# Weighting expert outputs before they are stored, and adding them to X inside the gathering transfers

## The chip, the cores and the metric

The program runs on one core of a Trainium2 chip. The metric is device time in microseconds (us). Six things work side by side: TensorE (PE in the profile; its weight loads are PEld), VectorE (DVE), ScalarE (ACT), GpSimd (POOL), SyncE (SP), which issues transfers, and 16 DMA engines. Transfers issued by SP appear in the profile as queue q1, those issued by ACT as q10 and those issued by POOL as q0. Each engine works through its instructions in order, and semaphores tie the engines together.

## What is computed

The model has two layers on X, 2048 tokens (4 sequences of 512) of 512 values. Each layer adds a state-space block and a feed-forward block to X. The feed-forward block of the first layer is a mixture of experts, and this is the part that the change touches:

```
router_logits = x @ gate_w.T                        # 16 experts
routing_weights = softmax(router_logits)
topk_w, topk_ids = top_k(routing_weights, 4)
def body(acc, ew):                                  # for each of the 16 experts e
    coef = sum(where(topk_ids == e, topk_w, 0.0), axis=-1)
    h = silu_and_mul(x @ w13_e.T)                   # 2 x 352 wide
    acc = acc + (h @ w2_e.T) * coef[:, None]
out = shared + sparse_out                           # shared: a dense expert, 1408 wide
```

The feed-forward block of the second layer quantizes its three weight matrices to -1, 0 or 1, with one scale per matrix (the mean absolute value of the whole matrix), and its activations to integers.

## The kernel before

Tokens stand in 16 tiles of 128 (`TT` = 16); X stays in SBUF as `X[128, 16, 512]` through the program. The program is a row of blocks, with a barrier and the clearing of that block's semaphores (`Mem.clear`) between two of them:

1. `ssm_first`: the state-space block of layer 0; beside it the expert weights are split into two half-precision parts.
2. `gate` for layer 0: multiplies by the gate, adds to X, normalizes, computes the router's logits.
3. `routing`: softmax, the four best experts of each token, and for each (token, choice) its place in a table of 80 x 128 slots (`NSTEP` = 80 steps of 128 slots, each step with one expert). DVE works out `r["pos"]`, the slot of each (token, choice), by a chain of small instructions. Then comes the inverse table `r["idx"]`, the token of each slot. It is built in a loop over the 64 pairs g of a token tile i and a choice k: DVE writes two one-hot matrices, `ohp` (L1007, 128 x 128, which row inside a step) and `ohs` (L1008, 128 x 80, which step, times the token's number), and PE adds their product to `pi` in PSUM (L1034). Four buffers of each let DVE run at most four pairs ahead; the semaphores are `oh_rdy` and `oh_used`. A float32 matmul is two passes in the trace, so 64 of them show as 128. Behind the loop DVE does some one-row arithmetic for the tables of weights (L1011 to L1019) and copies `pi` out (L1022).
4. `experts_and_ssm`: the shared expert and then 80 expert steps, with the state-space block of layer 1 spread over them. Step g fetches 128 tokens by `r["idx"]`, and its result stands in `py`. `y_evac(g)` on ACT (L1349) copies it to `yo` with a constant scale, and `y_store(g)` writes it to `y_d` in HBM, not weighted.
5. `combine`: two jobs that share a block. One is to add to X the 64 gathers, again one per pair g = (tile i, choice k), i outer: POOL issues an indirect transfer of 128 rows of `y_d` to one of 8 buffers `yr` (L1558), and DVE multiplies by the token's weight `w8` and adds to X (L1614). POOL waits for a free buffer (`used`), DVE for the landing (`got`). The other job quantizes the weights of layer 1: SP loads 12 pieces of 1 MB (L1550), DVE sums the magnitudes of each (L1592), then come the three totals (L1597), a matmul over partitions (L1566) and the scales (L1601, L1603); only then can the pieces be converted, each by ACT (L1571), DVE (L1607, `clip`) and ACT (L1581). DVE's order between the two jobs is written out by hand: a magnitude after each of the gathers 1 to 12, then a clip after every third.
6. `gate` for layer 1, and `quant_ffn`, the last block, which needs X, the quantized weights and their scales.

## Time and profile before

| what | us |
|---|---|
| three runs | 2286.73, 2280.6, 2284.96; median 2284.96 |
| the profiled execution, its own time | 2281.42 |
| its span, first to last instruction | 2279.2 |
| `routing`, by the trace | 723.3 to 785.3 |
| `experts_and_ssm` | 785.3 to 1906.0 |
| `combine` | 1906.0 to 2029.5 |
| `gate` and `quant_ffn` of layer 1 | 2029.5 to 2279.2 |

The profiled execution lies 3.5 us under the median of the runs, and its own time is 2.2 us over its span. Over the whole span the page gives PE 74% busy, DVE 77%, ACT 52% and POOL 59%, so no engine is the limit of everything. The blocks follow each other with barriers; a block's time is set by what ends last in it, and what a block gains or loses is passed on to the end.

### The profile page before, as it was taken

How to read it: one execution, taken by the hardware profiler on the slowest of the kernel's cores; microseconds unless marked ns; L12 is line 12 of the kernel's file. 1: busy time of each engine (PE TensorE's matmuls, PEld its weight loads, DVE VectorE, ACT ScalarE, POOL GpSimd, SP SyncE). 2: the span in 40 equal slices, each digit the busy share in tenths (PEclk: the TensorE clock that was granted, in tenths of full speed). 3: DMA queues.
4: the chain of work that ended last, by engine and by line, in shares of the span. 5: the costliest groups of instructions: out<-in, count | busy, mean ns of one | idle time of the engine just before them, and what ended most of it. 6: DMA issues, size and time to landing. Idle time of an engine off the chain costs nothing. (4 is left out here: it accounts for less than half of the span.)

```text
span 2279.2 us, 27596 instructions
## 1 busy us (share of the span) xinstructions
PE 1683.4 (74%) x8608; PEld 967.8 (42%) x8630; DVE 1759.7 (77%) x2275; ACT 1184.7 (52%) x1829; POOL 1336.8 (59%) x648
## 2 busy tenths in 40 slices
PE   4766756656536488999799988999889992005998
PEld 1222222212225445766467545666456661003554
DVE  4999999999955738887689847888478885757886
ACT  4675766757632034443444435555355551634776
POOL 0778778789950005775288815888258884653111
PEclk7878879889976588999899998999989996558999
DMA  6347456456544600001000333344424226650000
GB/s 213 132 149 236 149 169 222 152 177 223 182 143 134 144 24 10 11 13 35 5 10 30 135 113 137 121 157 159 144 95 157 81 75 249 210 170 1 24 24 28
DMA packets 127146, 264.65 MB, mean 116 GB/s; under 512 B 44546, under 2 KB 48386, under 8 KB 121794
## 3 DMA queue, kind: packets, MB, share of 16 engines
q1 hardware_dynamic: 93890, 184.24, 24.0%
q0 software_dynamic: 11520, 37.76, 5.8%
q10 hardware_dynamic: 21600, 40.90, 4.8%
q8 instruction: 78, 1.28, 0.2%
q14 instruction: 58, 0.48, 0.1%
HBM read 180.41 MB, written 82.44 MB: 115 GB/s over the span
## 5 line engine op out<-in xcount | busy, mean ns | idle before, releaser
L471 POOL TENSOR_TENSOR ssm_hs<-ssm_hs,ssm_Cs 128x1024 f32<-128x1024 f32 x128 | 314.9, 2461 | 144.7 <-DVE ssm_hs L434 140.7
L471 POOL TENSOR_TENSOR moe_hs<-moe_hs,moe_Cs 128x1024 f32<-128x1024 f32 x128 | 302.2, 2361 | 127.2 <-DVE moe_hs L434 96.1
L434 DVE TENSOR_TENSOR_SCAN moe_hs<-moe_dA,moe_bu 128x1024 f32<-128x1024 f32 x128 | 292.6, 2286 | 17.9 <-ACT moe_dA L348 8.4
L434 DVE TENSOR_TENSOR_SCAN ssm_hs<-ssm_dA,ssm_bu 128x1024 f32<-128x1024 f32 x128 | 292.8, 2287 | 17.4 <-ACT ssm_dA L348 0.5
L461 POOL TENSOR_TENSOR moe_U<-moe_U,moe_hs 128x1024 f32<-128x1024 f32 x128 | 302.0, 2360 | 5.9
L280 PE MATMUL ssm_pY<-ssm_hs,ssm_ident 128*128 128x512 f32 x512 | 276.9, 668 | 2.8 <-POOL ssm_hs L471 2.8
L1246 PE MATMUL moe_pgu<-all_Wreg,moe_xth 128*128 x1280 | 249.6, 318 | 31.4 <-DVE moe_xtl L1446 31.3
L1196 PE MATMUL moe_pgu<-moe_xsh,all_Wreg 128*128 128x256 f16 x1408 | 251.8, 277 | 10.9 <-DVE moe_hsl L1434 9.4
L258 PE MATMUL ssm_pB<-ssm_bc,ssm_sel 96*128 96x512 bf16 x128 | 54.9, 429 | 204.4 <-DVE ssm_bu L425 204.3
L1196 PE MATMUL moe_pgu<-moe_xsl,all_Wreg 128*128 128x256 f16 x704 | 195.0, 277 | 0.0
L666 POOL TENSOR_TENSOR ssm_wlo<-ssm_wst,ssm_whi 128x1360 f16<-128x1360 f32 x64 | 186.5, 2915 | 0.0
L348 ACT ACTIVATE ssm_dA<-ssm_dlt,ssm_A 128x511 f32<-128x511 f32 x256 | 169.0, 709 | 24.2 <-DVE ssm_hs L434 24.1
L348 ACT ACTIVATE moe_dA<-moe_dlt,moe_A 128x511 f32<-128x511 f32 x256 | 169.9, 714 | 18.3 <-DVE moe_du L413 18.3
L1246 PEld LDWEIGHTS moe_pgu<-all_Wreg,moe_xth 128*128 128x128 f16 x1280 | 127.0, 99 | 103.2 <-issue 36.9
L602 ACT ACTIVATE ssm_whi<-ssm_wst 128x1360 f16<-128x1360 f32 x64 | 85.5, 1336 | 155.4 <-DMA ssm_wst<-in_w_all 155.4
L425 DVE TENSOR_TENSOR ssm_bu<-ssm_du,ssm_pB 128x1024 f32<-128x1024 f32 x128 | 157.1, 1227 | 10.9 <-PE ssm_pB L258 0.8
L453 POOL TENSOR_TENSOR moe_U<-moe_U,moe_Dv 128x2048 f32<-128x2048 f32 x4 | 14.4, 3602 | 256.6 <-DVE moe_du L413 256.6
L425 DVE TENSOR_TENSOR moe_bu<-moe_du,moe_pB 128x1024 f32<-128x1024 f32 x128 | 156.3, 1221 | 6.8 <-PE moe_pB L258 6.7
L1196 PEld LDWEIGHTS moe_pgu<-moe_xsh,all_Wreg 128*128 128x128 f16 x1408 | 140.0, 99 | 40.6 <-issue 13.8
L280 PEld LDWEIGHTS ssm_pY<-ssm_hs,ssm_ident 128*128 128x128 f32 x512 | 111.2, 218 | 94.2 <-issue 85.2
L1246 PE MATMUL moe_pgu<-all_Wreg,moe_xtl 128*128 x640 | 150.3, 317 | 0.0
L1149 POOL DMA_INDIRECT moe_xg<-xn_d,all_idx x80 | 78.7, 983 | 120.7 <-PE moe_px L1219 110.3
(238 smaller groups left out, 3622.5 us busy)
## 6 DMA issues: line engine op xcount, KB each, us to landing
ssm_wst<-in_w_all SPq DMA_DIRECT2D x64, 680.0 KB, 4.9
w_hi<-ssm_whi SPq DMA_DIRECT2D x64, 340.0 KB, 2.3
w_lo<-ssm_wlo SPq DMA_DIRECT2D x64, 340.0 KB, 3.1
y_d<-moe_yo ACTq DMA_DIRECT2D x80, 256.0 KB
all_Wreg<-w_hi SPq DMA_DIRECT2D x16, 1088.0 KB
all_Wreg<-w_lo SPq DMA_DIRECT2D x16, 1088.0 KB
ssm_Cs<-c_d SPq DMA_DIRECT2D x64, 256.0 KB, 5.5
gate_Y<-y_ssm ACTq DMA_DIRECT2D x8, 1024.0 KB, 9.4
```

The source lines that it names most:

```text
L258: self.nc.tensor.matmul(self.pB[:], self.sel[:, ds(n, 1), :], self.bc3[:, b % self.dbl, :], start=True, stop=True).then_inc(self.b_rdy, 1)
L280: mm = self.nc.tensor.matmul(self.pY[k][:], self.ident[:], self.hs[:, j, k, :], start=False, stop=last, skip_group_check=True)
L348: ex = nc.scalar.activation(self.dA[:, q, k, 1:L], self.dlt[:, b % self.dbl, c, 1:L], ACT.Exp, scale=self.A[:, c, ds(n, 1)])
L425: self.nc.vector.tensor_tensor(self.bu[:], self.du[:, b % self.dbl, half * HC:(half + 1) * HC, :], self.pB[:].unsqueeze(1).to_broadcast([P ...
L434: self.nc.vector.tensor_tensor_scan(self.hs[:, j, :, :].rearrange("p k t -> p (k t)"), self.dA[:, q, :, :].rearrange("p k t -> p (k t)"), ...
L461: self.nc.gpsimd.tensor_tensor(Y, Y, self.hs[:, j, :, :], ALU.add).then_inc(self.acc_done, 1)
L471: self.nc.gpsimd.tensor_tensor(self.hs[:, j, :, :], self.hs[:, j, :, :], self.Cs[:, i:i + 1, :].to_broadcast([P, HC, L]), ALU.mult)\
L602: nc.scalar.activation(whi[:, k, :], wst[:, k, :], ACT.Copy, scale=WS).then_inc(hi_rdy, 1)
L666: nc.gpsimd.tensor_tensor(wlo[:, j % 2, :], wst[:, j % 2, :], whi[:, j % 2, :], ALU.subtract).then_inc(lo_rdy, 1)
L1149: nc.gpsimd.indirect_dma_start(out=xg[:, g % 2, :], out_offset=None, in_=r["xn_d"], in_offset=bass.IndirectOffsetOnAxis(ap=r["idx"][:, g:g ...
L1196: mm = nc.tensor.matmul(pgu[u % 2][:, q * TS:(q + 1) * TS], Ws[:, shared_place(c), z, o:o + P], xs[:, t % 2, k, :], start=(k == 0 and z == ...
L1246: mm = nc.tensor.matmul(ps, xt[:, k, :], w_of(w, z, P, k * 2 * IE + o, IE), start=(k == 0 and z == 0 and xt is xth), stop=(k == HK - 1 and ...
```

## The change

Expert outputs are stored already weighted. For that, `routing` gets a third one-hot matrix, `ohw` (step, times the weight), which POOL writes for each of the 64 pairs, and PE a second matmul per pair that adds its product with `ohp` to `pws`; DVE scales it to `r["wslot"]`, the weight of each slot. `y_evac` takes its scale from there, one value per partition, in place of the constant. In `combine` the buffers `yr` and DVE's multiply-and-add are gone: the gathers have X as their destination and add to it in the transfer (`compute_op=ALU.add`). Their order is now k outer, i inner, and the gather of (k, i) waits for the one of (k - 1, i), since both change the same tile of X. POOL waits for all of them at the end. DVE's order in `combine` is 12 magnitudes, totals, scales, 12 clips. SP's loads of weights are the same, in the same order. There are 2 more semaphores in `routing` and 7 more in `combine` (16 `got` for 8, and no `used`).

```
@@ routing
+        ohw = m.sb("ohw", [P, 4, NSTEP])
+        pws = m.ps("pws", [P, NSTEP])
...
-                V.tensor_copy(stf[:], sti[:])
+                V.tensor_copy(stf[:], sti[:]).then_inc(st_rdy, 1)
...
                 own(V.tensor_copy(r["idx"][:], pi[:]))
+                own(V.tensor_scalar(r["wslot"][:], pws[:], 1.0 / (HS * WS), None, ALU.mult))
...
                 for g in range(G):
                     pe.wait_ge(oh_rdy, g + 1)
-                    nc.tensor.matmul(pi[:], ohp[:, g % 4, :], ohs[:, g % 4, :], start=(g == 0),
+                    nc.tensor.matmul(pi[:], ohp[:, g % 4, :], ohs[:, g % 4, :], start=(g == 0), stop=(g == G - 1))
+                    pe.wait_ge(ow_rdy, g + 1)
+                    nc.tensor.matmul(pws[:], ohp[:, g % 4, :], ohw[:, g % 4, :], start=(g == 0),
                                      stop=(g == G - 1)).then_inc(oh_used, 1)
+
+            @block.gpsimd
+            def _(pool):
+                pool.wait_ge(loaded, 112)
+                pool.wait_ge(st_rdy, 1)
+                for g in range(TT * TOPK):
+                    i, k = g // TOPK, g % TOPK
+                    if g >= 4:
+                        pool.wait_ge(oh_used, g - 3)
+                    nc.gpsimd.tensor_scalar(ohw[:, g % 4, :], col[:, 0:NSTEP], stf[:, i, k:k + 1], r["w8"][:, i, k:k + 1],
+                                            ALU.is_equal, ALU.mult).then_inc(ow_rdy, 1)
@@ experts_and_ssm, y_evac
-                    nc.scalar.activation(yo[:, g % 2, :], py[:], ACT.Copy, scale=1.0 / (HS * WS)).then_inc(py_read, 1)
+                    nc.scalar.activation(yo[:, g % 2, :], py[:], ACT.Copy,
+                                         scale=r["wslot"][:, g:g + 1]).then_inc(py_read, 1)
@@ combine, POOL
-                for g in range(TT * TOPK):
-                    i, k = g // TOPK, g % TOPK
-                    if g >= NR:
-                        pool.wait_ge(used, g - NR + 1)
-                    nc.gpsimd.indirect_dma_start(
-                        out=yr[:, g % NR, :], out_offset=None, in_=r["y_d"],
-                        in_offset=bass.IndirectOffsetOnAxis(ap=r["pos"][:, i, k:k + 1], axis=0)).then_inc(got[g % NR], 16)
+                for k in range(TOPK):
+                    for i in range(TT):
+                        if k:
+                            pool.wait_ge(got[i], 16 * k)
+                        nc.gpsimd.indirect_dma_start(
+                            out=X[:, i, :], out_offset=None, in_=r["y_d"],
+                            in_offset=bass.IndirectOffsetOnAxis(ap=r["pos"][:, i, k:k + 1], axis=0),
+                            compute_op=ALU.add).then_inc(got[i], 16)
+                for i in range(TT):
+                    pool.wait_ge(got[i], 16 * TOPK)
@@ combine, DVE
-                for g in range(TT * TOPK):
-                    i, k = g // TOPK, g % TOPK
-                    dve.wait_ge(got[g % NR], 16 * (g // NR + 1))
-                    if k:
-                        dve.wait_ge(used, g)
-                    V.scalar_tensor_tensor(out=X[:, i, :], in0=yr[:, g % NR, :], scalar=r["w8"][:, i, k:k + 1],
-                                           in1=X[:, i, :], op0=ALU.mult, op1=ALU.add).then_inc(used, 1)
-                    if 1 <= g <= NP:
-                        magnitude(g - 1)
-                    if g == NP:
-                        total()
-                    if g == NP + 2:
-                        scales()
-                    if NP + 4 <= g < 4 * NP + 4 and g % 3 == 1:
-                        clip((g - NP - 4) // 3)
+                for n in range(NP):
+                    magnitude(n)
+                total()
+                scales()
+                for n in range(NP):
+                    clip(n)
```

How instructions stand on the engines that the prediction speaks of. First PE in `routing`, before:

```order
L1029 MATMUL rt_pr<-rt_M,rt_tri 128x256
L1030 MATMUL rt_pc<-rt_M,rt_ones 128x256
L1034 MATMUL rt_pi<-rt_ohs,rt_ohp 128x80 x64
```

and after:

```order
L1034 MATMUL rt_pr<-rt_M,rt_tri 128x256
L1035 MATMUL rt_pc<-rt_M,rt_ones 128x256
L1039 MATMUL rt_pi<-rt_ohs,rt_ohp 128x80
L1041 MATMUL rt_pws<-rt_ohw,rt_ohp 128x80
L1039 MATMUL rt_pi<-rt_ohs,rt_ohp 128x80
L1041 MATMUL rt_pws<-rt_ohw,rt_ohp 128x80
```

The 64 matmuls in a row become 64 alternating pairs, each pair from the same `ohp`. DVE in `combine`, the start of the block and then the end of the clips, before:

```order
L1614 SCALAR_TENSOR_TENSOR all_X<-comb_yr,all_w,all_X 128x512 x2
L1592 TENSOR_REDUCE comb_wsum<-comb_W 128x1
L1614 SCALAR_TENSOR_TENSOR all_X<-comb_yr,all_w,all_X 128x512
L1592 TENSOR_REDUCE comb_wsum<-comb_W 128x1
...
L1607 TENSOR_SCALAR comb_W<-comb_W 128x2048
L1614 SCALAR_TENSOR_TENSOR all_X<-comb_yr,all_w,all_X 128x512 x3
L1607 TENSOR_SCALAR comb_W<-comb_W 128x2048
L1614 SCALAR_TENSOR_TENSOR all_X<-comb_yr,all_w,all_X 128x512 x14
```

and the whole of it after:

```order
L1607 MEMSET comb_rnd 128x1
L1608 MEMSET comb_rnd 128x1
L1612 TENSOR_REDUCE comb_wsum<-comb_W 128x1 x12
L1617 TENSOR_REDUCE comb_wtot<-comb_wsum 128x3
L1621 TENSOR_SCALAR all_wsc<-comb_pa 128x3
L1623 RECIPROCAL comb_inv<-all_wsc 128x3
L1627 TENSOR_SCALAR comb_W<-comb_W 128x2048 x12
```

Nothing of the gathers is left on DVE; POOL alone carries them.

## Rows read from the trace of the kernel before

**Rows 1.** Busy time by stretch; (x) counts instructions, PEclk is the granted clock.
```profile
core 0: us, PE busy (x) PEld busy (x) DVE busy (x) ACT busy (x) POOL busy (x), PEclk, DMA share, GB/s
750.10:777.90 27.80, 27.63 (x128) 27.41 (x128) 27.80 (x128) 0.00 (x0) 0.00 (x0) 0.50 0.64 113
785.30:1906.00 1120.70, 1011.09 (x6288) 647.01 (x6288) 822.10 (x1062) 540.63 (x1067) 696.75 (x340) 0.95 0.24 81
```

**Rows 2.** A group of instructions of `routing`: busy us, mean ns | idle before, releaser.
```profile
L1034 PE MATMUL rt_pi<-rt_ohs,rt_ohp 128*128 128x80 f32 x128 | 27.6, 422 | 11.0 <-DVE rt_ohs L1008 11.0
```

**Rows 3.** Timeline of `routing`, its first one-hot matrix and its end: start us, us.
```profile
749.60 0.29 DVE L1007 TENSOR_SCALAR rt_ohp<-rt_col,rt_pp 128x128 f32<-128x128 f32 x1
...
776.53 1.27 PE L1034 MATMUL rt_pi<-rt_ohs,rt_ohp 128*128 128x80 f32 x5
776.73 0.30 DVE L1008 TENSOR_SCALAR rt_ohs<-rt_col,rt_stf,rt_tok 128x80 f32<-128x80 f32 x1
783.41 0.24 DVE L1022 CAST all_idx<-rt_pi 128x80 uint32<-128x80 f32 x1
```

**Rows 4.** Groups of instructions in `combine`.
```profile
L1558 POOL DMA_INDIRECT comb_yr<-y_d,all_pos x64 | 72.9, 1139 | 55.3 <-DVE all_X L1614 30.0 <-POOLq L91 12.8 <-issue 12.5
L1614 DVE SCALAR_TENSOR_TENSOR all_X<-comb_yr,all_w,all_X 128x512 f32<-128x512 f32 x64 | 47.8, 749 | 27.5 <-DMA comb_yr<-y_d,all_pos 26.7
L1571 ACT ACTIVATE comb_W<-comb_W,comb_rnd,comb_inv 128x2048 f32<-128x2048 f32 x12 | 24.9, 2080 | 61.3 <-DVE comb_inv L1603 61.3
L1581 ACT ACTIVATE all_Wq<-comb_W,comb_rnd 128x2048 bf16<-128x2048 f32 x12 | 23.9, 1993 | 3.8 <-DVE comb_W L1607 3.8
```

**Rows 5.** Timeline of `combine`, the instructions at its turning points.
```profile
1937.44 2.29 DVE L1592 TENSOR_REDUCE comb_wsum<-comb_W 128x1 f32<-128x2048 f32 x1 [0.24 <-DMA comb_W<-in_w_up]
...
1953.21 2.29 DVE L1592 TENSOR_REDUCE comb_wsum<-comb_W 128x1 f32<-128x2048 f32 x1 [0.22 <-DMA comb_W<-in_w_down]
...
1957.60 2.09 ACT L1571 ACTIVATE comb_W<-comb_W,comb_rnd,comb_inv 128x2048 f32<-128x2048 f32 x1 [61.26 <-DVE comb_inv L1603]
...
2006.50 2.00 ACT L1581 ACTIVATE all_Wq<-comb_W,comb_rnd 128x2048 bf16<-128x2048 f32 x1 [2.46 <-DVE comb_W L1607]
...
2024.70 0.75 DVE L1614 SCALAR_TENSOR_TENSOR all_X<-comb_yr,all_w,all_X 128x512 f32<-128x512 f32 x1 [0.76 <-DMA comb_yr<-y_d,all_pos]
```

**Rows 6.** Timeline: POOL's first gathers, one beside a clip; last, a group of `quant_ffn`.
```profile
1906.69 0.98 POOL L1558 DMA_INDIRECT comb_yr<-y_d,all_pos  x1 [12.84 <-POOLq L91]
1907.98 0.95 POOL L1558 DMA_INDIRECT comb_yr<-y_d,all_pos  x1 [0.30 <-issue]
...
1982.91 1.53 POOL L1558 DMA_INDIRECT comb_yr<-y_d,all_pos  x1 [0.30 <-issue]
1983.11 1.22 DVE L1607 TENSOR_SCALAR comb_W<-comb_W 128x2048 f32<-128x2048 f32 x1
...
L1812 POOL TENSOR_SCALAR ffn_xq<-ffn_xn 128x512 bf16<-128x512 f32 x16 | 30.7, 1921 | 154.9 <-ACT ffn_xn L1768 154.9
```

**Rows 7.** DMA issues of `combine`: median us from issue to landing.
```profile
comb_yr<-y_d,all_pos POOLq DMA_INDIRECT x64, 3.8
```

**Rows 8.** Groups of ACT in 1400 to 1800 us, each shape apart.
```profile
L1349 ACT ACTIVATE moe_yo<-moe_pys 128x512 f32<-128x512 f32 x54 | 32.3, 598 | 19.3 <-PE moe_pys L1227 19.3
L324 ACT ACTIVATE moe_hs<-moe_bu,moe_db 128x512 f32<-128x512 f32 x4 | 2.8, 688 | 1.5 <-PE moe_bu L250 1.5
```

**Rows 9.** DMA queues, packets, MB, share of 16 engines, in 1912 to 1930 us.
```profile
q1 hardware_dynamic: 707, 5.14, 69.7%
q0 software_dynamic: 707, 2.31, 32.1%
```

**Rows 10.** DMA queue, packets, MB, share of 16 engines, in 1940 to 1948 us.
```profile
q1 hardware_dynamic: 1234, 2.46, 83.9%
```

**Rows 11.** Busy time in two stretches of the block ahead, `gate`.
```profile
700.00:704.00 4.00, 4.00 (x39) 4.00 (x38) 3.78 (x14) 1.11 (x3) 0.00 (x0) 1.00 0.23 85
706.60:713.60 7.00, 7.00 (x36) 7.00 (x35) 0.61 (x2) 0.62 (x2) 0.00 (x0) 0.50 0.31 111
```

More of the change, by code:

```diff
@@ L910, in routing @@
         oh_rdy = m.sem("oh_rdy")
+        ow_rdy = m.sem("ow_rdy")
+        st_rdy = m.sem("st_rdy")
         oh_used = m.sem("oh_used")
@@ L1515, in combine @@
         m = Mem(nc, ctx, "comb")
-        NR = 8
         NP = 3 * 4
-        yr = m.sb("yr", [P, NR, H])
         W = m.sb("W", [P, NP, IF])
@@ L1525, in combine @@
         pa = m.ps("pa", [P, 4])
-        got = [m.sem(f"got{i}") for i in range(NR)]
-        used = m.sem("used")
+        got = [m.sem(f"got{i}") for i in range(TT)]
         w_in = [m.sem(f"w_in{i}") for i in range(NP)]
@@ L1890, in bass_program @@
             "idx": m.sb("idx", [P, NSTEP], U32),
+            "wslot": m.sb("wslot", [P, NSTEP]),
             "tab": m.sb("tab", [1, 2, NSTEP], I32),
```

## The prediction

> **What bounds the kernel now.** Blocks are divided by barriers, so I read block by block which chain ends last; the change touches three. First the busy times by stretch and the groups of `routing` [rows 1, 2]. In the loop over 64 pairs, 27.8 us long, both DVE (27.80) and PE (27.63) are busy all the time. DVE starts `ohp` at 749.60 and the last `ohs` at 776.73 [rows 3], which is 0.43 us a pair; PE has two passes a pair, 27.6 us / 128 = 0.2155 us a pass, or 0.43 us a pair, at granted clock 0.50, the lower level of 1.2 GHz. The two are tied, neither has room. Behind the loop DVE alone needs 6.4 us for one-row arithmetic, until `idx` at 783.41.
>
> In `experts_and_ssm` the reader is to see PE at 1011 of 1121 us, at clock 0.95, and ACT at 541 [rows 1]: PE sets the pace there.
>
> In `combine` there are two chains [rows 4, 5]. The weights: SP issues the loads from the block's start, the eighth piece is there at 1937.4 and the twelfth at 1953.2 (DVE waited for both); 4.4 us later (1957.60) ACT starts to convert and ends at 2006.50 + 2.00 = 2008.5. The gathers: the last multiply-and-add ends at 2024.70 + 0.75 = 2025.45. So the gathers end last, 17 us behind the conversion. They are late since POOL waited 30.0 us in total for DVE to free buffers, and DVE had them between its magnitudes. An issue takes POOL 0.95 us and 0.30 us of gap [rows 6], and the rows land 3.8 us behind it [rows 7]; so 64 of them need 80 us if nothing holds them.
>
> **Routing: a second matmul per pair.** Removed: nothing. Added: on PE 64 matmuls of the shape of L1034, 128 passes x 0.2155 = 27.6 us. PE has no gap in the loop, and there is no other work of PE in this block, so all of it lies on the path as long as the clock stays at 0.50. I take it to stay: 27.8 us of uninterrupted passes of this same kind left it at 0.50 [rows 1], and the new loop has the same passes, only twice as many. The loop's PE part ends at 750.2 + 64 x 0.862 = 805.4. DVE may write its last pair when PE has done the sixtieth, at 750.2 + 60 x 0.862 = 801.9, and ends it 0.5 us later at 802.4, where it ended at 777.0: 25.4 us later. The one-row arithmetic then still hides PE's last passes (802.4 + 6.4 = 808.8, after 805.4). The added `wslot` instruction costs 0.2 (as the copy beside it, 0.24 [rows 3]). Sum: **+25.6 us**.
>
> POOL's 64 `ohw` stand in no row. The nearest is TENSOR_SCALAR on 128 x 512, 1.92 us [rows 6]. By elements, 80 of 512 is 0.30 us; by instruction it is 1.92 at most. It hides if it stays under the 0.862 us that PE needs; I take about 0.4, between them and near the first, since an instruction that touches a sixth of the elements is nearer to the count of elements than to the whole, and keep 1.92 as the far end. POOL is idle in this block and nothing is queued behind it.
>
> **Experts: a scale per partition.** L1349 takes 598 ns with a constant scale; L324, also from PSUM, with an operand per partition takes 688 [rows 8]. At most 80 x 0.09 = 7 us on ACT, at least nothing. ACT waits 19.3 us for PE in front of just this instruction within 54 steps, and has half its time free, PE being the bound [rows 1, 8], so the cover is ample; only the last two lie open: +0.2. If ACT had no slack, 7 us.
>
> **Combine: DVE is freed, and POOL with it.** Removed from DVE: 64 x 0.749 = 47.8 us [rows 4], which was on the path of the gathers. Gathers now run at POOL's pace, up to 16 in flight where there were 8. What is late next? Not the gathers, if POOL issues every 1.25 us: 1906.7 + 80 + 4 to land = 1991. It is the weights, because the gathers now press on the loads. In 1912 to 1930, when gathers were queued, q0 and q1 each had 707 packets: they take turns packet by packet [rows 9]. A q1 packet of that stretch costs 0.697 x 18 x 16 / 707 = 0.284 us of an engine, a q0 packet 0.321 x 18 x 16 / 707 = 0.131. For the first eight loads there are 9 packets an engine each (128 rows of 8 KB and the completion): 72 x (0.284 + 0.131) = 29.9 us, from 1907.5 to 1937.4, which is the landing seen [rows 5]. The last four loads have rows of 2 KB, 33 packets an engine each; such a packet costs 0.839 x 8 x 16 / 1234 = 0.087 [rows 10]. Before, POOL was held back there, and they took 15.8 us. Now q0 always has something queued: 132 x (0.087 + 0.131) = 28.8 us, so the last weight lands at **1966.2**, 13 us later than today.
>
> From there to ACT's start it was 4.4 us, of which about 0.6 was a multiply-and-add between total and scales: 3.8. Then ACT has 24.9 + 23.9 = 48.8 us without a wait, as clips no longer stand behind gathers: 1966.2 + 3.8 + 48.8 = 2018.8, against 2025.45: **-6.6 us**. The whole of this rests on an accumulating packet costing what a plain one does. The rows hold no accumulating transfer. Bounds: at the cheap end POOL's larger appetite doesn't matter either (slightly slower issue gives the loads more of the engines, at best as today, 1953.2 + 52.6 = 2005.8, -19.6); at the dear end both the row and X are read, twice the engine time. I take the plain price because it is the only measured one.
>
> Nine more semaphores to clear: from the last DVE instruction to the next block (the table of blocks) it is 1.65 us with 9 semaphores in `routing` and 4.05 with 30 in `combine`, so at most 0.12 each; between nothing and 1.0 I take +0.5.
>
> **Sum** against the profiled execution: 2281.4 + 25.6 + 0.2 - 6.6 + 0.5 = 2301.1. The median of the runs is 3.5 us higher: **2304.6**.
>
> **Rival 1, the transfers that add take twice the engine time.** For: an add must read X as well as the gathered row. Then the first eight loads take 72 x (0.284 + 0.262) = 39.3 us, to 1946.8, the last four 132 x (0.087 + 0.262) = 46.1, to 1992.9, and ACT ends at 2045.5: combine +20.0 in place of -6.6, 2331.2. The block becomes slower than today when the last weight lands behind 2025.45 - 52.6 = 1972.85, which is 65.35 us of loading; q1's own packets take 72 x 0.284 + 132 x 0.087 = 31.9 of it, so the point is at 33.4 / 204 = 0.164 us for a q0 packet, against 0.131 today. 
>
> **Rival 2, POOL's issue becomes the chain.** An adding gather may need more descriptors, up to twice 0.95 us. At 1.9 + 0.3 = 2.2 us the 64 need 141 us and end at 1906.7 + 141 + 4 = 2051.7: combine +26.2, 2337.4. It decides from (2018.8 - 4 - 1906.7) / 64 = 1.69 us an issue, and makes the block slower than today from 1.79. The same holds if the transfers themselves go one by one more slowly than that.
>
> **Rival 3, the routing loop is covered (not slower).** If the longer loop brings the clock to its upper level, a pass takes half, 0.108 us; uninterrupted float32 passes at clock 1.00 are in the trace, 4.00 us for 39, beside 7.00 us for 36 at 0.50 [rows 11]. Then PE needs 0.43 us a pair, again tied with DVE, and the routing costs about 1: 2304.6 - 24.6 = 2280, no change. Against: the loop today.
>
> **Rival 4, POOL sets the routing loop.** From 0.862 us an `ohw` POOL is the bound. A clip on DVE stretches POOL's issue from 0.95 to 1.53 [rows 6], so DVE's TENSOR_SCALAR of float32 can hold POOL up. With DVE's 0.43 in front of a POOL instruction of 0.8 us it is 1.23 us a pair, 64 x 0.37 = +24, 2328. The far end of 1.92 us would be 64 x 1.06 = +68; I leave it outside the range, within this rival's chance.
> The Trainium skill, "SBUF — State Buffer", "Who interferes with whom", says that such a VectorE instruction in its two-port mode shuts GpSimd out until it ends; the stretched issue agrees with it. At my 0.4 us the sum, 0.83, would just stay hidden.
>
> **Chances.** Forecast (routing +25, combine between -20 and +4) 0.47; rival 1 0.20; rival 2 0.15; rival 3 0.08; rival 4 0.05; slower adds than any bound here 0.05. The routing term is the firm one and stands in all but rival 3, so nearly all cases are slower. Range: down to 2304.6 - 14 = 2290 it takes in most of the cheap end of the loads, up to rival 2 with some spare, 2342; outside are rival 3, the slowest adds and a little of either. A difference of 0.3% (6.9 us, so 2278.1 to 2291.8) is about what a measurement of this kernel can tell from no change: faster 0.04 (rival 3 with cheap adds), same 0.09, slower 0.87.
>
> **What would show it.** Right: 256 passes of about 0.215 us in the routing loop at clock 0.50, the block 25 us longer; POOL's `ohw` under 0.86 us; as many packets of q0 as of q1 while weights load, the wait of the last magnitude ending near 1992 (1966 moved by 25.6), ACT without gaps and last in `combine`. Wrong: a wait of PE on POOL in the loop; the last gather landing after ACT's end; a weight landing beyond 2000; clock 1.00 in the loop; or a wait of PE for ACT's `y_evac`.

## The result, and the profile after

The changed kernel takes 2320.27 us (median of 4 runs, 2319.57 to 2321.24) beside 2284.05 us of the kernel before on the same chip: 1.0157 times as long, 95% interval 1.0144 to 1.0169, so 36.2 us slower. The forecast was 19.6 us slower. All three changed blocks end later than before; the one gain that was forecast, in `combine`, is a loss.

First the busy times by stretch, the changed kernel's blocks from the start of one to the start of the next: `routing`, `experts_and_ssm`, `combine`, and the rest (`gate` for the second time and `quant_ffn`). Of all executions in this document one, of the kernel e7 below, took 8023.84 us beside 2261.87 to 2269.9 for its other five; it has no trace, and e7's median is that of the five.

```profile
core 0: us, PE busy (x) PEld busy (x) DVE busy (x) ACT busy (x) POOL busy (x), PEclk, DMA share, GB/s
726.22:813.87 87.65, 56.95 (x260) 55.86 (x260) 57.79 (x238) 3.21 (x4) 49.64 (x64) 0.50 0.52 102
813.87:1937.27 1123.40, 1012.52 (x6288) 647.28 (x6288) 822.12 (x1062) 547.24 (x1067) 696.65 (x340) 0.95 0.24 81
1937.27:2069.64 132.37, 0.56 (x2) 0.50 (x2) 42.77 (x29) 46.63 (x24) 101.67 (x64) 0.50 0.99 222
2069.64:2318.20 248.56, 198.27 (x1130) 103.92 (x1152) 182.11 (x407) 156.97 (x198) 50.45 (x32) 0.90 0.10 35
```

The kernel before, cut the same way:

```profile
723.30:785.30 62.00, 29.67 (x132) 28.59 (x132) 51.83 (x237) 3.21 (x4) 0.00 (x0) 0.50 0.70 144
785.30:1906.05 1120.75, 1011.09 (x6288) 647.01 (x6288) 822.10 (x1062) 540.63 (x1067) 696.75 (x340) 0.95 0.24 81
1906.05:2029.53 123.48, 0.56 (x2) 0.50 (x2) 86.58 (x93) 47.11 (x24) 72.91 (x64) 0.50 0.71 238
2029.53:2279.20 249.67, 198.87 (x1130) 103.75 (x1152) 182.05 (x407) 157.07 (x198) 50.47 (x32) 0.91 0.10 35
```

The differences are +25.65, +2.65, +8.89 and -1.11 us, 36.1 together. That this is so near the distance of the medians is in part chance: the two profiled spans lie 39.0 us apart, because of one more difference ahead of `routing`, in code that both kernels share. The weight loads of the last 32 matmuls of the first `gate` take 4.18 us in the one trace and 6.95 in the other, at different granted clocks (before, then after):

```profile
717.00:721.00 4.00, 4.00 (x33) 3.91 (x32) 0.00 (x0) 0.59 (x1) 0.00 (x0) 0.90 0.00 0
...
717.20:724.00 6.80, 6.74 (x33) 6.62 (x32) 0.00 (x0) 0.61 (x2) 0.00 (x0) 0.50 0.00 0
```

A granted clock of 1.00 is 2.4 GHz and 0.50 is 1.2. Which clock these matmuls get does not hang on the change: the block takes 70.9 us in the kernel before and 73.8 in the changed one, and of the experiments below 73.8 in e7 and e8 and 67.6 in e10, which have the routing of the kernel before, and 71.0 in e1, which has the new one. I leave it out of every comparison and compare blocks.

**`routing`.** Both matmuls of a pair, and POOL's one-hot matrix (the last line: min/median/max ns, first and last start), to hold against [rows 2, 3]:

```profile
L1039 PE MATMUL rt_pi<-rt_ohs,rt_ohp 128*128 128x80 f32 x128 | 40.7, 422 | 11.0 <-DVE rt_ohs L1012 11.0
L1041 PE MATMUL rt_pws<-rt_ohw,rt_ohp 128*128 128x80 f32 x128 | 40.6, 421 | 0.0
...
781.00:795.00 14.00, 14.00 (x67) 14.00 (x67) 8.57 (x34) 0.00 (x0) 13.04 (x17) 0.50 0.01 2
...
L1052 POOL TENSOR_SCALAR rt_ohw<-rt_col,rt_stf,all_w x64: 624/793/821, 752.6 to 804.7; 128x80 f32<-128x80 f32 x64
```

A pass has still 422 ns from its start to its end and starts every 0.21 us (67 in 14 us); PE has no gap, and the granted clock is 0.50 throughout. POOL is nearly as busy, with 0.79 us an instruction and one every 0.85.

**`combine`.** The timeline of POOL, DVE and ACT at the places that answer to [rows 5, 6]; the last line is of all 64 gathers:

```profile
1937.92 1.60 POOL L1575 DMA_INDIRECT all_X<-y_d,all_pos  x1 [13.04 <-POOLq L91]
1939.83 1.56 POOL L1575 DMA_INDIRECT all_X<-y_d,all_pos  x1 [0.30 <-issue]
...
1999.75 2.29 DVE L1612 TENSOR_REDUCE comb_wsum<-comb_W 128x1 f32<-128x2048 f32 x1 [5.24 <-DMA comb_W<-in_w_down]
...
2003.45 4.08 ACT L1591 ACTIVATE comb_W<-comb_W,comb_rnd,comb_inv 128x2048 f32<-128x2048 f32 x2 [75.95 <-DVE comb_inv L1623]
...
2042.08 1.72 POOL L1575 DMA_INDIRECT all_X<-y_d,all_pos  x1 [0.30 <-issue]
2044.11 1.55 POOL L1575 DMA_INDIRECT all_X<-y_d,all_pos  x1 [0.30 <-issue]
...
2046.21 3.88 ACT L1601 ACTIVATE all_Wq<-comb_W,comb_rnd 128x2048 bf16<-128x2048 f32 x2
...
2057.25 1.55 POOL L1575 DMA_INDIRECT all_X<-y_d,all_pos  x1 [0.30 <-issue]
...
DMA to landing us min/median/max: 5.3/15.8/24.4
```

The reader is to see which chain ends last. The twelfth weight is there at 1999.75, 62.5 us after the block's start, ACT follows 3.7 us later and ends at 2050.1. POOL starts every gather 0.30 us behind the end of the one before and waits for no transfer beyond that, but an adding gather takes it 1.55 us where a plain one took 0.95; with the gap of 0.30 it is 1.85, and beside a clip of DVE 2.02; on the average a gather starts every 1.89 us. The 64 issues last until 2058.8, 8.7 us after ACT's end, and the next block starts at 2069.64. That is rival 2 of the forecast, and one of the forecast's own signs of being wrong (the last gather landing after ACT's end).

### The profile page after: what moved, and what is told of

Same layout as the page of the kernel before. It is cut to its first block and busy times, and to the rows that moved or that the text cites. A ratio compares the mean times of both kernels' runs of the same rounds, so it can differ in the third digit from the quotient of the medians.

```text
span 2318.2 us, 27824 instructions
## 1 busy us (share of the span) xinstructions
PE 1719.9 (74%) x8736; PEld 1000.3 (43%) x8758; DVE 1721.9 (74%) x2212; ACT 1190.5 (51%) x1829; POOL 1415.0 (61%) x712
## 3 DMA queue, kind: packets, MB, share of 16 engines
q8 instruction: 79, 1.29, 0.2%
## 5 line engine op out<-in xcount | busy, mean ns | idle before, releaser
L1245 PE MATMUL moe_pys<-all_Wreg,moe_hth 128*128 (+1 forms) x480 | 145.7, 385 | 1.4 <-DVE moe_htl L1471 1.4
```

The lines of the kernel that those rows point to most:

```text
L1245: mm = nc.tensor.matmul(py[:], ht[0:n, q, :], w_of(w, z, n, HK * 2 * IE + q * H, H), start=(q == 0 and z == 0 and ht is hth), stop=(q == 2 ...
```

## The experiments

Twelve kernels ran, each beside the kernel before on the same chip. The block times are read from their traces, cut at the same places as above.

### Which part of the change costs what (e1, e2)

e1 is the kernel before with `routing` of the changed one, `wslot` computed and read by nobody:

```diff
@@ routing as in the changed kernel; y_evac and combine as before
+            "wslot": m.sb("wslot", [P, NSTEP]),
```

> The kernel before with only the routing of the change: ow one-hots on POOL, second matmul, wslot; nobody reads wslot, y_evac and combine are as before. Theory (the costs sit in their blocks and add): routing 62.0 -> 87.6 us, combine stays 123.5, and experts_and_ssm is some 2.5 us longer (1123.4 instead of 1120.8) although y_evac is untouched, because that excess arose in the first 85 us of the block, where the granted clock was lower; sum about 2284 + 25.6 + 2.5 = 2312. Rival (the excess of the experts comes from y_evac's scale operand): experts_and_ssm 1120.8, sum 2309.6. Second rival (the 25 us arise only together with something else of the change): under 2305.

e2 is the kernel before with `combine` of the changed one and nothing else:

```diff
@@ combine as in the changed kernel; routing and y_evac as before
```

> The kernel before with only the combination of the change (adding gathers). The routing weights are left out, so the rows are added unweighted; number and size of transfers and instructions are those of the change. Theory (POOL's issue is the chain that ends last): 64 issues of 1.55 us and 0.30 of gap, combine 132.4 instead of 123.5 us, sum about 2284 + 8.9 = 2293. Rival (the block is slower because of something the longer routing does): combine near 123.5, sum 2284.

Measured: e1 2310.27 us against 2283.77 (ratio 1.0122, 1.0096 to 1.0148), e2 2289.97 against 2283.77 (1.0037, 1.0023 to 1.0051). The blocks, of e1 `routing`, experts, `combine`, then of e2 `combine`:

```profile
724.77:812.27 87.50, 56.94 (x260) 55.86 (x260) 57.66 (x238) 3.21 (x4) 49.71 (x64) 0.50 0.52 102
812.27:1934.90 1122.63, 1012.01 (x6288) 647.31 (x6288) 822.07 (x1062) 540.66 (x1067) 696.97 (x340) 0.95 0.24 81
1934.90:2058.47 123.57, 0.56 (x2) 0.50 (x2) 86.58 (x93) 47.16 (x24) 72.93 (x64) 0.50 0.71 238
...
1906.69:2038.50 131.81, 0.56 (x2) 0.50 (x2) 42.76 (x29) 46.63 (x24) 101.69 (x64) 0.50 0.99 223
```

The costs sit in their blocks. e1 has the +25.5 of the routing and an unchanged `combine`; e2 has +8.3 in `combine` alone. The 26.5 and 6.2 us of the two medians make 32.7 of the 36.2; the rest is within their intervals. e1 also has 1.9 of the 2.65 us in the experts, where its ACT does exactly the work of before (540.66 us busy). So most of that term is not `y_evac`'s scale. It arises at the block's start: ACT's first `moe_dA` came 82.6 us after the start before and 85.1 in the changed kernel, and from there to the end the block is as long as before. In the first 45 us the granted clock was 0.73 before, 0.71 in e1 and 0.70 in the changed kernel. A lower clock fits the longer start; no experiment changed it alone, so as a cause it is argued and not shown.

### Why `combine` is slower (e3, e4, e9)

e3 takes the addition out of the gathers; the rows overwrite X:

```diff
                         nc.gpsimd.indirect_dma_start(
                             out=X[:, i, :], out_offset=None, in_=r["y_d"],
-                            in_offset=bass.IndirectOffsetOnAxis(ap=r["pos"][:, i, k:k + 1], axis=0),
-                            compute_op=ALU.add).then_inc(got[i], 16)
+                            in_offset=bass.IndirectOffsetOnAxis(ap=r["pos"][:, i, k:k + 1], axis=0)).then_inc(got[i], 16)
```

> The changed kernel with plain gathers into X: the rows overwrite X and the addition is left out. Theory (adding makes the issue and the packets dear): an issue 0.95 us and 0.30 gap, q0 back to 11520 packets, last gather landed some 85 us after the block's start, the last weight at about 60 us (the forecast's own number for plain-priced packets), ACT without gaps ends the block: 112.8 + 4.6 = 117.4 us instead of 132.4, sum 2320.3 - 15 = 2305. Rival (the issue is long because the rows land in X, or because the queue is full, not because they are added): issue stays 1.55 us and the block 132.4, sum 2320.

e4 keeps the addition and halves the row:

```diff
-                            out=X[:, i, :], out_offset=None, in_=r["y_d"],
+                            out=X[:, i, 0:H // 2], out_offset=None, in_=r["y_d"].rearrange("r (a h) -> (r a) h", a=2),
```

> The changed kernel with adding gathers of half the row (256 of 512 elements, from y_d seen as rows of half the length; the other half of the sum is left out). Theory (POOL's issue per gather sets the block, whatever a row's size): issue still 1.55 + 0.30 us, combine 130 to 133 us though the engines move half the gathered bytes; the last weight lands earlier than the 62.5 us of the change. Rival (the DMA engines' time per byte sets the block, and the issue only reflects a full queue): the interval from issue to issue falls clearly below 1.85 us and the block to 115 to 120 us.

Measured: e3 2301.69 us against 2283.77 (1.0079, 1.0061 to 1.0098), which is 18.6 below the changed kernel; e4 2319.77. The blocks and POOL's issues (ns min/median/max, first and last start), first e3, then e4:

```profile
1936.35:2049.93 113.58, 0.56 (x2) 0.50 (x2) 42.75 (x29) 46.63 (x24) 64.10 (x64) 0.50 0.70 259
...
L1575 POOL DMA_INDIRECT all_X<-y_d,all_pos x64: 942/946/1770, 1937.0 to 2019.3; - x64
...
1938.49:2068.57 130.08, 0.56 (x2) 0.50 (x2) 42.76 (x29) 46.63 (x24) 101.67 (x64) 0.50 0.70 162
...
L1575 POOL DMA_INDIRECT all_X<-y_d,all_pos x64: 1540/1549/2144, 1939.1 to 2058.5; - x64
```

Both decide for POOL's issue: without the addition the issue is back at 0.95 us although the rows land in the same X; with half the bytes it stays at 1.55, and the block is only 2.3 us shorter although the mean DMA share falls from 0.99 to 0.70 and the last weight came 49.5 us into the block instead of 62.5. e3 is at the same time the forecast's own case, adding at the price of plain transfers: the last weight was waited for until 1996.99, 60.6 us into the block (the working said 60.2), ACT started 3.7 us behind it, and the block took 113.6 us where the working gives 117.4 (112.8 to ACT's end and 4.6 to the next block). The 3.8 us between are ACT, which needed 46.6 us for what I had put at 48.8, and the end of the block: 2.6 us from ACT's end to the next block, where 4.6 were put.

The Trainium skill, "Perfetto Trace Analysis", "DMA Instruction — SWDGE (GPSIMD)", says that the profiled end of such an instruction on GpSimd is the moment when its cores have generated the descriptors, not when data have moved. e4 agrees: half the bytes, the same 1.55 us. So I asked whether the price goes by the number of pieces. The queue counts them (packets, MB, share), first the changed kernel, then e3, whose packets are as many as those of the kernel before:

```profile
q0 software_dynamic: 15616, 37.76, 7.4%
q0 software_dynamic: 11520, 37.76, 5.2%
```

The difference is 64 gathers times 64, so an engine gets 9 packets for an adding gather (8 rows and the completion) and 5 for a plain one. e9 adds only 64 rows a gather:

```diff
-                            out=X[:, i, :], out_offset=None, in_=r["y_d"],
-                            in_offset=bass.IndirectOffsetOnAxis(ap=r["pos"][:, i, k:k + 1], axis=0),
+                            out=X[0:P // 2, i, :], out_offset=None, in_=r["y_d"],
+                            in_offset=bass.IndirectOffsetOnAxis(ap=r["pos"][0:P // 2, i, k:k + 1], axis=0),
```

> The changed kernel with adding gathers of 64 rows instead of 128 (partitions 0 to 63; the sums of the other tokens are left out). Theory (POOL's issue pays per packet: with the plain gather at 5 packets an engine and 0.95 us and the adding one at 9 and 1.55 us, it is 0.20 us fixed and 0.15 per packet): 64 rows are 4 packets and the completion, 5 an engine, an issue takes 0.95 us and the gathers end after 64 x 1.25 = 80 us; ACT then ends the block near 110 us, sum about 2300. Rival (an adding gather has a fixed dearer issue, whatever the number of rows): issue 1.55, block 130 us, sum 2319.

Measured: 2311.12 us against 2284.93. The block and POOL's issues, then q0:

```profile
1936.68:2062.75 126.07, 0.56 (x2) 0.50 (x2) 44.03 (x29) 46.63 (x24) 95.78 (x64) 0.50 0.70 167
...
L1575 POOL DMA_INDIRECT all_X<-y_d,all_pos x64: 1412/1421/2072, 1937.3 to 2050.9; - x64
...
q0 software_dynamic: 11520, 29.37, 5.6%
```

The packets fell to 5 an engine as expected, the issue only to 1.42 us. My theory that the packets make the whole price falls: four packets an engine and 64 rows are worth 0.13 us together, and with as many packets as a plain gather the adding one still takes 0.47 us more, for half the rows. How much of the 0.6 us does not depend on the rows at all is an estimate: if the 0.13 us for 64 rows go on in a straight line, an adding issue without rows would take 1.29 us, at least 0.34 above a plain one of 128 rows; a plain gather of 64 rows was not run. What POOL does in this time, no run shows.

**What the adding transfers cost the DMA engines.** Rival 1 said twice the engine time for what is moved. The rows of the two queues while the last weights load (packets, MB, share of 16 engines), first the changed kernel in 1970 to 2000 us, then e3 in 1975 to 1995, then the changed kernel in 2000 to 2020, where only gathers are left:

```profile
q0 software_dynamic: 2154, 3.92, 70.7%
q1 hardware_dynamic: 1992, 3.95, 39.0%
...
q0 software_dynamic: 1467, 4.81, 62.5%
q1 hardware_dynamic: 1464, 2.93, 41.3%
...
q0 software_dynamic: 2237, 4.08, 112.5%
```

Per MB on q0 an engine was occupied 0.707 x 30 x 16 / 3.92 = 86.6 us with adding and 0.625 x 20 x 16 / 4.81 = 41.6 us with plain transfers: 2.1 times. The rule of the Trainium skill named in the forecast (both sources are read through the same ring, half the rate) agrees with that in its factor; its reason no row here shows. The loads hardly paid for it, though. The two queues got nearly as many packets each (2154 to 1992, 1467 to 1464), so they take turns by packet here, and an adding packet holds one row: it is 0.158 us of an engine, where a plain one of two rows is 0.136. So a load waits hardly longer at each turn, and the last weight came 62.5 us into the block instead of 60.6. The factor 2 falls on the gathers alone, and they hide it under POOL's 1.85 us.

They could not hide much more. In 2000 to 2020 the engines are busy all the time, and 2237 packets in 20 us are 0.143 us each; 64 gathers of 9 packets an engine are 82 us, and the loads' own packets 31.9 (the forecast's number). Together 114 us, close behind POOL's 121. By this estimate from the rows a cheaper issue alone would win some 7 us; that was not tried.

**The end of the block (e11).** From the end of the last issue to the next block it is 10.8 us. The last gather landed 6.1 us after the start of its issue (its row is the one below), which is 4.6 after its end; so 6.3 us lie between the landing and the next block. The forecast had 8.05 for the whole, 4 to land and 4.05 to clear.

```profile
all_X<-y_d,all_pos POOLq DMA_INDIRECT x1, 6.1
```

In e11 the 16 last waits move from POOL to SP:

```diff
+                for i in range(TT):
+                    sp.wait_ge(got[i], 16 * TOPK)
...
-                for i in range(TT):
-                    pool.wait_ge(got[i], 16 * TOPK)
```

> The changed kernel with the 16 waits for the last gathers moved from POOL to SP. From the end of the last issue to the next block it was 10.8 us, where landing took some 4 of them; the forecast had about 8 (4 to land, 4.05 to clear). Theory (POOL is slow in passing 16 waits and the barrier): the tail shrinks to 8 to 9 us, sum 2318. Rival (the last adding transfers land that late and the rest is the clearing of 41 semaphores): the tail stays 10.8 us, sum 2320.

Measured: 2319.38 us against 2283.09 (1.0149, 1.0131 to 1.0167), the tail 9.5 us (last issue ends 2058.39, next block 2067.87). It went in the direction of the theory by 1.3 us, to a value between the two that were expected (8 to 9, and 10.8), and the medians don't tell the two kernels apart. The number of semaphores (37; the 41 of the expectation is a miscount) does not set the tail: e3 has as many, and its next block starts 2.6 us after ACT's last instruction. Where the rest of the tail is spent stays open.

### What sets the routing loop (e5, e6, e12)

e5 writes both one-hot matrices side by side into one tile, so that PE does one matmul a pair, of 160 columns; POOL still writes the second half:

```diff
-                    nc.tensor.matmul(pi[:], ohp[:, g % 4, :], ohs[:, g % 4, :], start=(g == 0), stop=(g == G - 1))
                     pe.wait_ge(ow_rdy, g + 1)
-                    nc.tensor.matmul(pws[:], ohp[:, g % 4, :], ohw[:, g % 4, :], start=(g == 0),
+                    nc.tensor.matmul(pi[:].rearrange("p z n -> p (z n)"), ohp[:, g % 4, :],
+                                     ohs[:, g % 4, :, :].rearrange("p z n -> p (z n)"), start=(g == 0),
                                      stop=(g == G - 1)).then_inc(oh_used, 1)
```

> The changed kernel with the two one-hots side by side in one tile of 160 columns, so that one matmul a pair gives both the token numbers and the weights: 128 passes in the loop instead of 256. POOL still writes the weighted half. Theory A (PE's second pass alone lengthens the loop): about 0.43 to 0.55 us a pair, routing 62 to 70 us instead of 87.6, sum 2296 to 2303. Theory B (POOL's one-hot of 0.79 us with its gap of 0.05 is as slow as PE's two passes and sets the loop by itself): 0.84 us a pair, routing 86 to 87.5, sum 2319.

e6 is e5 with the second half written by ACT (POOL's loop is left out):

```diff
+                for g in range(TT * TOPK):
+                    i, k = g // TOPK, g % TOPK
+                    act.wait_ge(oh_rdy, g + 1)
+                    nc.scalar.activation(ohs[:, g % 4, 1, :], ohs[:, g % 4, 0, :], ACT.Copy,
+                                         scale=r["w8"][:, i, k:k + 1]).then_inc(ow_rdy, 1)
```

> As e5_one_pass, but ScalarE writes the second half of the tile, as a copy of the token half times the weight (so what the weights compute is changed: token number times weight; the output is not that of the reference). POOL has nothing to do in the loop. Theory A and B alike expect the loop to be set by DVE and PE: about 0.43 to 0.55 us a pair, routing 62 to 70 us; the number tells what 160 columns cost a pass. If it stays above 0.8 us a pair, neither PE's passes nor POOL were the limit but the longer chain from DVE over a second engine to PE with four buffers.

Measured: e5 2307.83 us and e6 2294.49, both against 2283.59. First e5's block `routing`, its PE group and POOL's, then e6's block and its experts:

```profile
727.62:803.49 75.87, 36.12 (x132) 22.01 (x132) 57.48 (x238) 3.21 (x4) 43.42 (x64) 0.75 0.59 118
...
L1038 PE MATMUL rt_pi<-rt_ohs,rt_ohp 128*128 128x160 f32 x128 | 34.1, 363 | 20.5 <-POOL rt_ohs L1050 16.7
...
L1050 POOL TENSOR_SCALAR rt_ohs<-rt_col,rt_stf,all_w x64: 626/672/1802, 753.9 to 796.7; 128x80 f32<-128x80 f32 x64
...
727.70:791.30 63.60, 30.66 (x132) 22.77 (x132) 52.98 (x238) 26.34 (x68) 0.00 (x0) 0.71 0.72 140
791.30:1911.77 1120.47, 1010.02 (x6288) 646.48 (x6288) 822.18 (x1062) 547.69 (x1067) 696.45 (x340) 0.95 0.24 81
```

e5 lies between the two theories. PE waits for POOL (16.7 us), whose matrices take 0.67 us each (median), so POOL is the next bound, but not at 0.84 us a pair. With POOL out of the loop the block is 63.6 us, 1.6 above the kernel before: the weights as such are cheap, if they ride in the same pass, at the granted clock that e6 had. e6 also has `y_evac` with the scale operand (ACT 547.69 us busy) and the experts at 1120.47, no longer than before: with e1, which has the longer block without the operand, this shows that `y_evac`'s operand costs nothing.

What I had not expected is the column of the granted clock, 0.75 and 0.71 where it was 0.50. In stretches of e6 from 754.5 on:

```profile
754.50:759.00 4.50, 3.94 (x15) 3.97 (x16) 4.25 (x19) 3.23 (x9) 0.00 (x0) 0.50 1.26 230
759.00:765.00 6.00, 5.97 (x28) 4.75 (x27) 5.94 (x27) 4.61 (x14) 0.00 (x0) 0.84 0.86 132
765.00:771.00 6.00, 6.00 (x29) 4.18 (x29) 6.00 (x29) 5.08 (x15) 0.00 (x0) 1.00 0.87 151
```

So e5's gain of 11.8 us could be the missing passes or the clock. e12 is e5 with the wide matmul done twice, 256 passes again:

```diff
+                    both = ohs[:, g % 4, :, :].rearrange("p z n -> p (z n)")
+                    nc.tensor.matmul(pi[:].rearrange("p z n -> p (z n)"), ohp[:, g % 4, :], both,
+                                     start=(g == 0), stop=(g == G - 1))
+                    nc.tensor.matmul(pws[:].rearrange("p z n -> p (z n)"), ohp[:, g % 4, :], both,
+                                     start=(g == 0), stop=(g == G - 1)).then_inc(oh_used, 1)
```

> As e5_one_pass (both one-hots in one tile of 160 columns, POOL writes the weighted half), but PE does the wide matmul twice a pair, so again 256 passes in the loop, now of 160 columns. In e5_one_pass and e6_one_pass_act the granted clock rose from 0.50 to 1.00 within the loop, in the changed kernel with 256 passes of 80 columns it stayed at 0.50. Theory C (the clock that the loop is granted decides; the wide passes raise it): clock 1.00 from about 760 us on, the passes at about half of 0.26 us each, the loop set by POOL's 0.65 us a pair, routing 76 to 79 us, sum about 2308 to 2312. Theory D (the number of passes decides): clock stays at 0.50, four... no, 256 passes of 0.26 us, 1.05 us a pair, routing near 100 us, sum above 2328.

Measured: 2309.79 us against 2283.09 (1.011, 1.0093 to 1.0127). The block, then a stretch of the loop, and last the same stretch of e5:

```profile
727.96:805.66 77.70, 46.23 (x260) 40.21 (x260) 57.68 (x238) 3.21 (x4) 44.33 (x64) 0.76 0.58 115
...
770.00:780.00 10.00, 10.00 (x63) 8.61 (x63) 7.80 (x31) 0.00 (x0) 10.00 (x16) 1.00 0.32 64
762.00:786.00 24.00, 24.00 (x150) 20.93 (x149) 19.30 (x75) 0.00 (x0) 24.00 (x37) 1.00 0.40 69
...
762.00:786.00 24.00, 18.51 (x73) 10.88 (x74) 18.91 (x74) 0.00 (x0) 24.00 (x37) 1.00 0.39 69
```

Theory C holds: as many passes as in the changed kernel, each twice as wide, and the block is 10 us shorter, with a clock that rose to 1.00, as in e5 and e6. 63 passes of 160 columns in 10 us are 0.16 us each, where a pass of 80 columns at clock 0.50 takes 0.21. What sets the loop then is POOL: in 24 us it writes 37 matrices without a gap, 0.65 us each, in e12 and in e5 alike, though e12 has twice the passes. So in the changed kernel it is PE's narrow passes at the lower clock that set the 25 us, with POOL's 0.65 a pair behind them; with POOL as the bound, in e5, 13.9 of the 25.65 us are still there (75.87 against 62.00).

### Taking the work off DVE in another way (e7, e8, e10)

e3 showed that `combine` is 10 us shorter than before when POOL and ACT are not held up by DVE (and DVE's additions are left out). That needs no adding transfer: in the kernel before, ACT waits 61 us for the scales with nothing to do [rows 4]. e7 keeps the plain gathers and DVE's multiply-and-add, gives the 12 magnitudes to ACT, and 6 of the 12 first conversions to DVE, which shares them out between its last 22 additions:

```diff
-        NR = 8
+        NR = 14
...
+                for n in range(NP):
+                    act.wait_ge(w_in[n], 16)
+                    if n:
+                        act.wait_ge(abs_rdy, n)
+                    nc.scalar.activation(Wq[n // 4][:, n % 4, :], W[:, n, :], ACT.Abs,
+                                         accum_out=wsum[:, n // 4, n % 4:n % 4 + 1]).then_inc(abs_rdy, 1)
...
+                            V.tensor_scalar(W[:, step - 100, :], W[:, step - 100, :],
+                                            inv[:, (step - 100) // 4:(step - 100) // 4 + 1], ROUND,
+                                            ALU.mult, ALU.add).then_inc(dv_rdy, 1)
```

> The kernel before with another way to take work off DVE in combine: plain gathers, multiply-and-add on DVE as before, 14 buffers instead of 8, the 12 magnitudes on ScalarE (which waits there anyway), and 6 of 12 first conversions on DVE. Theory (what held up the block was DVE, in front of the buffers and of the rounding): POOL issues at 1.25 us throughout, last weight near 60 us, ACT behind it 12 x 1.99 + 6 x 2.08 = 36.4 us, the block ends near 102 to 106 us instead of 123.5; sum 2284 - 19 = 2265. Rival (the loads, delayed by the faster gathers, eat the gain): last weight beyond 70 us and the block over 115 us, sum above 2276.

e8 is the kernel before with only the ring changed, e10 is e7 with the ring of before:

```diff
-        NR = 8
+        NR = 14
```

> The kernel before with 14 buffers for gathered rows instead of 8 and nothing else. Theory (DVE's own work, 90 us of it, is the chain, buffers are only where POOL feels it): the block shortens by the waits of DVE for gathers late in the block, at most 9 us (26.7 in total, most of it at the start and on weights), sum 2277 to 2284. Rival (the number of buffers was the limit): the gathers end at 85 us and the block is set by ACT at about 103 + the later weights, 115 us or less, sum 2275 or less.

> As e7_best (magnitudes on ScalarE, 6 first conversions on DVE), but with the 8 buffers of the kernel before. Theory (with DVE free early in the block 8 buffers are enough except while DVE turns to the rounding): the block 106 to 110 us, sum 2265 to 2271. Rival (POOL is held back again by buffers while it should run ahead): last gather added after 112 us, sum above 2273.

Measured: e7 2265.94 us against 2283.59 (0.992, 0.9904 to 0.9936); e8 2283.61 against 2283.59 (1.0, 0.9989 to 1.0012); e10 2271.08 against 2284.93 (0.9943, 0.9926 to 0.996). The block `combine` of e7, e8 and e10, then e7's ACT and DVE at the end:

```profile
1905.88:2011.56 105.68, 0.56 (x2) 0.50 (x2) 69.23 (x87) 58.88 (x42) 75.12 (x64) 0.50 0.77 279
...
1908.30:2031.33 123.03, 0.56 (x2) 0.50 (x2) 87.22 (x93) 46.65 (x24) 77.07 (x64) 0.50 0.70 239
...
1904.75:2016.01 111.26, 0.56 (x2) 0.50 (x2) 68.68 (x87) 58.88 (x42) 77.45 (x64) 0.50 0.75 265
...
2002.57 5.77 ACT L1589 ACTIVATE all_Wq<-comb_W,comb_rnd 128x2048 bf16<-128x2048 f32 x3
...
2005.64 3.31 DVE L1620 SCALAR_TENSOR_TENSOR all_X<-comb_yr,all_w,all_X 128x512 f32<-128x512 f32 x4
```

ACT ends at 2008.3 and DVE at 2008.95: the two chains are even, and the block is 17.8 us shorter than before. The loads did not eat the gain, the last weight came 60.9 us into the block. Deeper buffers alone (e8) bring nothing: DVE's own work is still 87 us, and POOL still waits 22.5 us for DVE to free buffers (30.0 before). With DVE relieved the block is 5.6 us shorter with 14 buffers than with 8 (e7 against e10, one trace each); the medians are 3.8 us apart, each taken against the kernel before beside it, and their intervals overlap. e10's block of 111.3 us is a little above the 106 to 110 that were expected. e7 is faster than both kernels, by 18 and by 54 us.

## Why the prediction was right, and where it was not

**Direction and range** held: slower, and 2320.3 lies in 2290 to 2342. The direction rests on the routing term, which came as worked out. That the time lies in the range does not speak for the sum: its term for `combine` had the wrong sign, and the range holds because it reached up to rival 2, which had a chance of 0.15. The likeliest case gave 2304.6, 15.7 too low. In differences it said +19.6 where +36.2 were measured; 15.5 of the 16.6 us between them are the term of `combine`, 2.5 that of the experts, and the last blocks give 1.1 back.

**Routing, +25.6**: measured +25.65 in the changed kernel and +25.5 in e1. The step holds in its parts: 256 passes of 0.2135 us at clock 0.50 (0.427 a matmul), PE without a gap, the one-row arithmetic behind DVE's last pair. The assumption that the clock stays was right for passes of this shape; in the three kernels with passes of 160 columns it rose. So the clock can rise within such a loop, as rival 3 had it, and even so the loop would not have cost "about 1", as POOL's matrices hold it at 0.65 us a pair (13.9 us in e5).

**POOL's `ohw`, 0.4 us**: too low. It is 0.79 us paced by PE, and 0.65 in the loops that wait for it. The value was taken by the share of elements, from a row with 512; between the bounds of 0.30 and 1.92 it lies in the lower half, but further up than I put it. It cost nothing since it stayed under 0.862, by 0.07 us by its own duration. POOL as the bound was that near; e5, where PE waits 16.7 us for it, shows it as the next one. Rival 4's own sum, DVE's 0.43 in front of POOL's 0.8, did not come: in 14 us of the loop POOL is 13.04 us busy and DVE 8.57, so their recorded spans overlap.

**Experts, +0.2**: the block measured +2.65, but the term was right. ACT's instruction went from 598 to 686 ns, and the 7 us of added work were covered (e6). The 2.65 arise at the block's start, with a lower granted clock there, a cost that I had nowhere in the sum; e1 has 1.9 of it without any change to the experts.

**Combine, -6.6, measured +8.9**: here the sum failed. The failing step is the term "An issue takes POOL 0.95 us and 0.30 us of gap", carried over to adding gathers; they take 1.55. So the chain of the gathers, which the sum had landing at 1991, ends last, and ACT does not. I had put the threshold correctly: the issue decides from 1.69 us with its gap, and is slower than before from 1.79; it is 1.89, so the block is slower than before by little. Rival 2 was the right case, its price of 1.9 us for the issue too high and its chance of 0.15 too small, for no row spoke for the plain price either. The chain of the weights was worked out well: the last weight at 60.2, measured 60.6 with plain (e3) and 62.5 with adding transfers; ACT's end at 112.8, measured 112.8, although partly by two errors that cancel, 2.3 us more for the weight and 2.2 less for ACT.

**Rival 1, twice the engine time**: the mechanism is there (86.6 against 41.6 us per MB), the consequence is not. The reason against it that the forecast gives, packets cut one row each, is what the packet counts show.

**Semaphores, +0.5**: no run shows it. The tail from the last issue is 10.8 us where 8.05 were put, and e11 moved 1.3 of it; e3, with the same semaphores, has a tail of 2.6 us behind ACT, shorter than the 4.05 of the kernel before.

**The base**: the stretches of code that nobody touched moved by +2.8 us in the first `gate`, at a lower granted clock, and by -1.1 at the end, where the mean clock is nearly the same (0.91 before, 0.90 after) and the cause stays open.

## What to carry to other kernels

Here an instruction that was moved into a transfer had to be paid at the engine that issues it. Before trading a vector operation for an adding gather, compare the issue on POOL, not the bytes: here 64 times 0.75 us on a DVE that had other work to give away were traded for 64 times 0.6 us on the engine that became the chain. If an engine holds up a block, look first for one that waits in the same block: ACT stood idle for 61 us, and giving it DVE's magnitudes, together with half of the first conversions on DVE, won 14 us with 8 buffers and 18 with 14, where the adding transfers lost 9. And if a value must go through the same permutation as another one, put both side by side into one pass instead of adding a second.

## What the runs showed of the hardware that I had not expected

- An adding indirect gather of 128 rows takes POOL 1.55 us to issue, a plain one into the same tile 0.95. Half the bytes a row leave it at 1.55, half the rows bring it to 1.42. Beside a clip of DVE the plain one took 1.53 [rows 6], the adding one 1.72.
- An adding gather is cut into one packet a row (9 an engine), a plain one into one of two rows (5 an engine); per MB the adding one occupies an engine 2.1 times as long, yet delays the load queue that takes turns with it by only 3% (62.5 against 60.6 us).
- The granted clock stayed at 0.50 through 55 us of back-to-back float32 passes of 80 columns, and had risen to 1.00 by 765 us in a loop that began at 754.5 with passes of 160 columns (e6). It rose likewise in e12 and in e5, where PE even waits between its passes.
- POOL's TENSOR_SCALAR on 128 x 80 takes 0.65 to 0.79 us, a third to two fifths of the 1.92 on 128 x 512 [rows 6] for a sixth of the elements.
